# Batch 2's input load, first norm and first queries moved up in a hand-written instruction order

## The reference

```
x: (8, 512, 256);  mod = silu(c) @ wmod -> sa, ca, ga, sb, cb, gb per batch (ga, gb kept at least 0.25 from 0)
h = layernorm(x) * (1 + ca) + sa
x = x + ga * causal_attention(h, 16 heads of width 16)          # first attention
h = layernorm(x) * (1 + cb) + sb
xn = layernorm(h) * ln_g + ln_b
o = full_attention(xn, 32 heads of width 8) @ wo + h            # second attention
y = gelu(o @ w1[e] + b1[e]) @ w2[e] + b2[e]                     # an expert for each 256 tokens
out = x + gb * y
```

## Time and profile before

| | |
|---|---|
| time, median of 3 runs | 1482.61 us (1480.02 to 1482.8) |
| the profiled execution: time / its span | 1480.15 us / 1478.4 us |
| PE, DVE, ACT, POOL busy | 94%, 76%, 68%, 33% of the span |
| main steps 0, 4, 8, 12, 16 start (PE) | 60.42, 73.69, 87.72, 100.68, 113.77 us |
| granted TensorE clock | 0.999 |

### The profile page before, as it was taken

One profiled execution on the slowest core, in us unless ns is written; L12 is line 12 of the kernel. 1 busy time (PEld: TensorE's weight loads), 2 busy tenths in 40 slices (PEclk: granted clock), 3 DMA queues, 4 the chain that ended last, 5 costly groups with the idle time before them and its releaser, 6 DMA issues.

```text
span 1478.4 us, 29822 instructions
## 1 busy us (share of the span) xinstructions
PE 1395.2 (94%) x9588; PEld 592.0 (40%) x9588; DVE 1124.9 (76%) x2850; ACT 1007.1 (68%) x2094; POOL 489.2 (33%) x1242
## 2 busy tenths in 40 slices
PE   8888899998999999999999999999999989999998
PEld 5333333332443344433434334343344333343337
DVE  6777889988687878789687886868867797867721
ACT  4256567887767776767767676776766766786772
POOL 3345555332331434224341433415333133302100
PEclk9999999999999999999999999999999999999999
DMA  7776545545372645547365453735537341535240
GB/s 226 192 182 175 125 129 150 171 133 130 104 211 78 192 118 149 146 135 184 96 180 142 131 146 101 215 113 155 135 97 204 92 117 43 165 93 156 91 130 15
DMA packets 193887, 204.97 MB, mean 139 GB/s; under 512 B 58432, under 2 KB 143744, under 8 KB 193736
## 3 DMA queue, kind: packets, MB, share of 16 engines
q1 hardware_dynamic: 189960, 200.53, 49.9%
q10 hardware_dynamic: 3776, 2.53, 0.6%
HBM read 123.99 MB, written 79.02 MB: 137 GB/s over the span
## 4 chain that ended last, share of the span: by engine, by line
PE 76%; DVE 9%; ACT 8%; issue 3%; DMA 2%; SPq 1%; POOL 1%; ACTq 0%; DVEq 0%; POOLq 0%
PE bank_out L1596 18%; PE bank_scores L1574 14%; PE bank_max L1552 10%; PE bank_side L1513 8%; PE bank_side L1693 7%; PE bank_side L1526 4%; PE bank_max L1673 4%; ACT probs L1348 3%; DVE max_column L1822 3%; PE bank_side L1673 2%; PE bank_side L1634 2%; PE bank_scores L1673 2%; DVE bank_max L1819 2%; PE bank_side L1646 2%; ACT L1348 1%
## 5 line engine op out<-in xcount | busy, mean ns | idle before, releaser
L1348 ACT ACTIVATE probs<-bank_scores 128x512 f32<-128x512 f32 (+3 forms) x1536 | 753.1, 544 | 269.6 <-PE bank_scores L1574 264.0
L1822 DVE TENSOR_REDUCE max_column<-bank_max 128x1 f32<-128x512 f32 x1024 | 653.1, 682 | 96.0 <-PE bank_max L1552 91.7
L1596 PE MATMUL bank_out<-probs,v_tile 128*9 128x512 f32 (+4 forms) x3072 | 361.6, 542 | 5.4 <-ACT probs L1348 1.6
L1574 PE MATMUL bank_scores<-q_stack,k_stack 64*128 64x512 bf16 (+3 forms) x2048 | 313.9, 343 | 31.9 <-ACT probs L1348 29.7
L1552 PE MATMUL bank_max<-k_stack,q_stack 64*128 64x512 bf16 (+3 forms) x2048 | 308.4, 336 | 23.2 <-DVE max_column L1819 10.3
L1819 DVE CUSTOM_DVE_ANT_0 bank_max<-bank_max,causal 128x384 f32<-128x384 f32 (+3 forms) x512 | 241.8, 515 | 108.1 <-PE bank_max L1552 104.8
L1574 PEld LDWEIGHTS bank_scores<-q_stack,k_stack 64*128 64x128 bf16 x2048 | 81.0, 93 | 421.1 <-issue 415.2
L1178 POOL CAST max_parts<-max_row 128x32 bf16<-128x32 f32 x96 | 22.8, 237 | 386.9 <-DVE max_row L1835 386.0
L1552 PEld LDWEIGHTS bank_max<-k_stack,q_stack 64*128 64x128 bf16 x2048 | 101.8, 94 | 94.0 <-issue 60.6
L1693 PE MATMUL bank_side<-w_out,hidden_T 128*128 128x256 f32 x448 | 126.5, 405 | 0.0
L1196 POOL TENSOR_SCALAR_AFFINE_SELECT probs<-probs 128x512 f32<-128x512 f32 x128 | 81.6, 637 | 77.4 <-ACT probs L1348 76.8
(11 more groups left out here) (158 smaller groups left out, 1369.2 us busy)
## 6 DMA issues: line engine op xcount, KB each, us to landing
q_stack<-q_parts SPq DMA_DIRECT2D x124, 256.0 KB, 4.4
k_stack<-k_parts SPq DMA_DIRECT2D x124, 192.0 KB, 5.9
out_raw<-out_raw SPq DMA_DIRECT2D x74, 256.0 KB, 2.7
w_in<-in_L_ffn_w_dram SPq DMA_DIRECT2D x15, 1024.0 KB, 5.2
w_out<-in_L_ffn_w_dram SPq DMA_DIRECT2D x15, 1024.0 KB, 7.2
q_parts<-partsq SPq DMA_DIRECT2D x32, 384.0 KB, 3.1
k_parts<-partsk SPq DMA_DIRECT2D x32, 384.0 KB, 3.5
q_parts<-partsq SPq DMA_DIRECT2D x32, 256.0 KB, 3.1
```

The costliest lines, as they stand in the source:

```text
L1348: nc.scalar.activation(probs[s % 2][:, head_at(k), q0:S], region[bank][:, q0:S], ACT.Exp, scale=float(WIDTH[a]) ** -0.5).then_inc(drained[ ...
L1574: ins = pe.matmul(region[to][:, q0:S], k_stack[buf][rows, at, kt * P:(kt + 1) * P], q_stack[buf][rows, at, q0:S], start=(i == 0), stop=last)
L1596: ins = pe.matmul(outb[32 * k:32 * k + WIDTH[a] + 1, q0:S], v_tile[a][:, kt, g * GROUP + k, :], probs[s % 2][:, k, q0:S], start=(kt == 0), ...
L1822: v.tensor_reduce(dst, region[bank], AX_X, ALU.max).then_inc(drained[bank], 1)
```

## The change

Batch 2's `load_x` goes from slot 3 of the causal steps into the opening. Its norm up to the second of three Newton steps goes into the last slots of the lead-in, its normalising to slots 5 and 7 of the causal steps (the pieces stood in slots 7 to 27). Its two transposes go from slots 29 and 33 to 9 and 13, and its eight `qk` items from slots 37 to 65 to slots 17 to 45. No item is added or taken away.

```diff
@@ -438,13 +438,15 @@
-    second = [*v_items(0, 0), ("stacks", 0, 0), ("stacks", 0, 1), *norm_1[NEWTON_PIECE + 1:], *features_items(1, 0), ("idle_products", 0, 102), *qk_items(0, 1)[:4]]
+    second = [*v_items(0, 0), ("stacks", 0, 0), ("stacks", 0, 1), *norm_1[NEWTON_PIECE + 1:], *features_items(1, 0), ("load_x", 2), ("idle_products", 0, 102), *qk_items(0, 1)[:4]]
...
     place_at(beside, (20, 22, 24, 26), v_items(0, 1))
+    place_at(beside, (20, 22, 24, 24, 24, 24, 24), layernorm_items(2, 0)[:NEWTON_PIECE + 1])
+    place(beside, 27, [("newton", 2, 0, 1)])
@@ -457,14 +459,13 @@
     place_at(beside, (54, 88), [("blanks", 1, 0), ("blanks", 1, 1)])
-    place(beside, 3, [("load_x", 2)])
     place(beside, 10, [("stacks", 1, 0)])
     place(beside, 39, [("stacks", 1, 1)])
     place(beside, 40, [("load_gate", 0)])
-    place_norm(beside, (7, 10, 14, 15, 15, 15, 15, 25, 27), 2, 0)
-    place_at(beside, (19, 23), [("newton", 2, 0, 1), ("newton", 2, 0, 2)])
-    place_at(beside, (29, 33), features_items(2, 0))
-    place_at(beside, (37, 41, 45, 49, 53, 57, 61, 65), qk_items(0, 2))
+    place_at(beside, (5, 7), layernorm_items(2, 0)[NEWTON_PIECE + 1:])
+    place(beside, 0, [("newton", 2, 0, 2)])
+    place_at(beside, (9, 13), features_items(2, 0))
+    place_at(beside, (17, 21, 25, 29, 33, 37, 41, 45), qk_items(0, 2))
```

## The result

The changed kernel takes 1488.15 us (median of 5, 1486.64 to 1488.66) against 1482.43 (1480.02 to 1482.8): a ratio of **1.0043, 95% interval 1.0032 to 1.0053**. It is slower by 0.4%, 5.7 us where +1.1 was forecast, and outside the range. The profiled execution took 1488.52 us with a span of 1486.8.

The account below looks back on a forecast made before the run. PE's work was taken as the bound on average, with SP's queue and trip landings setting some steps. Step 16's +1.7 us (opening's 0.8 included) less 0.6 gave +1.1 us: 1483.7 us, 8-in-10 range 1479.9 to 1486.8.

Parts of the forecast that it names:

- Part 1, the load in the opening, +0.8: Opening: x_in ahead of trip 0's load on the full queue delays step 0 to 61.2 us, +0.8 us (0 to 1.4).
- Part 2, the norm, 0: Lead-in: some 2.5 us of norm work on DVE fits where DVE waits for PE, cost 0.
- Part 3, five products earlier: Steps 0 to 16: five qk fill PE's idle time; step 8 at 88.5, step 12 at 102.0, PE ready at 112.3.
- Part 4, the queue behind trip 2: SP's queue after trip 2: 2.49 MB instead of 0.92 delays trip 4's load to 113.7, step 16 to 115.5, +1.7 us.
- Part 5, steps 16 to 20, -0.6: Steps 16 to 20: one qk of 1.06 us leaves step 16, about half gained, -0.6 us (0 to -1.06).
- The rival of the clock (0.08): PE's clock falls to 1.2 GHz after the new 3.2 us wait before step 16: +4.3 us, 1486.9 us; chance 0.08.
- the queue is slower: Queue behind trip 2 runs at 275 GB/s, 9.1 instead of 6.8 us: +3.4 us in all, 1486.0 us; chance 0.12.

Follow-up runs that it names:

- kernel 2: The changed kernel with SP issuing batch 2's four stores of split queries and keys at their old slots, products still early: 1480.89 us, ratio 0.9996.
- kernel 3: The changed kernel with only the second two of batch 2's four part stores back at their old slots 57 and 65: 1482.33 us, ratio 1.0006.
- kernel 1: The kernel before with only batch 2's x_in load moved into the opening: 1483.02 us against 1481.92, ratio 1.0010.
- kernel 4: The changed kernel with the gate and bias loads (384 KB) moved from slot 40 to 66, behind trip 4's load: 1487.55 us, ratio 1.0036.
- kernel 6: The changed kernel with 22 matmuls of zeros on PE between steps 15 and 16: 1486.61 us, ratio 1.0034.
- kernel 5: The changed kernel with batch 2's four early part stores issued by ACT on its own queue, three slots behind the products: 1483.44 us, ratio 1.0015.
- 9: Kernel 2 with six more zero products on PE ahead of step 0: 1481.31 us, ratio 1.0002.
- 10: Kernel 8 with six more zero products on PE ahead of step 0: 1482.41 us, ratio 1.0002.
- kernel 7: Kernel 2 with batch 2's x_in load put ahead of batch 0's stack loads in SP's queue: 1480.26 us, ratio 0.9993.
- kernel 8: Kernel 2 with batch 2's x_in load in the opening issued by ACT instead of SP: 1481.26 us, ratio 0.9993.

## Why the prediction was wrong

**Direction, place and mechanism of the wait were right; its size was not, and the fall of the clock behind it was left out of the sum.** The forecast said +1.1 us, from a new wait before step 16 that the four early stores make through SP's queue. Kernels 2 and 3 show that chain. At step 20 the profile is some 6 us later than forecast: 1.0 from the opening, -0.9 from steps 0 to 12, 3.4 from steps 12 to 16 and 2.4 from steps 16 to 20.

- *Part 1, the load in the opening, +0.8.* The times of kernel 1 give +1.1 us, within its ends, but with an interval of 0.1 to 2.7. In the profile it is +1.8, from two sizes: trip 0's load went out at 59.93 and not at 59.4, and from that load to step 0 it takes 2.2 to 2.3 us in all ten profiles in which PE waits for it, not the 1.8 taken over from trip 2. So the slack before step 0 was 0.3 to 0.4 us and not 0.8.
- *Part 2, the norm, 0.* `x_in` landed at 53.0 us, and DVE's first statistic ran at 54.23. Nothing waited.
- *Part 3, five products earlier.* Step 8 was due at 88.5 and came at 89.0, step 12 at 102.0 and came at 102.09. That this fits is luck: the opening was 1.0 us late, and steps 0 to 8 and 8 to 12 took 0.5 and 0.4 us less than forecast. The text had step 8 still waiting for trip 2; it was PE's own work that set it (12.68 of 13.00 us busy, no wait for the trip). Steps 12 to 16 want 11.8 to 11.9 us (the changed kernel up to its wait, kernel 2), not 10.3, so PE was ready at 113.9 and not 112.3. Four items of 1.06 us taken away give back 13.09 - 11.9 = 1.2 us of 4.2; PE now waits in between for ACT's exponentials and DVE's maxima, 0.3 to 0.6 us at a time.
- *Part 4, the queue behind trip 2: the step that failed.* Trip 4's load was due at 113.7 and went out at 117.09, 3.4 us later. Of these, 1.0 is the opening and 0.7 is trip 3, whose load was due at 96.3 and went out at 98.04. The other 1.6 lie where the text says "From there to trip 4's store the order has the same bytes" and takes over the 15.1 us of the kernel before from the stack loads to trip 4's load; 16.7 passed (100.35 to 117.09). Two things in those 15.1 us did not carry over. Before, SP reached the store at 102.0 and waited until 103.5 for its rows, so 1.5 us of a delay should have vanished there; but SP now took 1.2 us longer to issue what stands between, the whole stretch without a pause. And the trip itself was taken at 5.7 us and took 7.6, of which 1.9 are the slower issue of its store. The second store of queries, put in just ahead of the stack loads and counted only with its 1.6 us of issue, had 768 KB in flight there, and kernels 3 and 4, with fewer bytes ahead of the trip, had it sooner. But how much of the 1.6 us these bytes are is open: kernel 2, with the order of before from trip 3 to trip 4, took 16.6 us for the same stretch, and the others with that order 15.9 to 16.8. The 15.1 of the one profile read is the shortest of them. The rate was not what failed: 0.7 us on the 6.8 of trip 3's 2.49 MB is about 330 GB/s (an estimate from these times), inside the bounds of 275 and 367. The rival *the queue is slower* named a trip 4 after 115 as its sign, and the sign came, but not from that stretch.
- *Part 5, steps 16 to 20, -0.6.* At full clock they take 14.59 instead of 14.99 in kernels 2, 3 and 6: -0.4.
- *The rival of the clock (0.08) came true beside the forecast.* It was priced at +3.2 us, and is 2.25 us (kernel 6). The wrong thing was the chance, and that it was treated as a case apart: the text forecast a wait of 3.2 us, and in kernel 4 the clock fell behind one of 3.03 us. With this term in the sum the forecast would have been some +3.4 us (1.1 + 2.25). The Trainium skill's rule cited there (TensorE: Matmul & The Clock Gate, Part 1) agrees with the rows at these waits: the same four matmuls took 1.03 us instead of 0.61 after 3.03 and 5.08 us of waiting, and 0.61 after 1.14 us. A single wait of PE does not explain all falls, though: in kernel 5 the clock fell with no wait above 0.95 us near it, and from 60 to 76 us it fell behind waits of 0 to 2.1 us (9 and 10).

The loss in the profiles by the parts: opening +1.8, steps 0 to 12 -0.4, the wait +3.8, the clock and step 16's missing product +1.85, together +7.1 at step 20. In the times, by the ratios of the kernels: the load +1.0 thousandths, the early norm and products -1.4, the first two stores +1.0, the second two +3.7 with the clock in it. The sum is +4.3, as measured, because it is made of the same ratios. The first has 0.9 of uncertainty, the others 1.2 to 1.4, so the first two stores' part alone is not shown by the times.

A version that surely beats the kernel before was not found. Kernels 7 and 8 have the lowest ratios, 0.9993, with 1 inside both intervals.

## What to carry to other kernels

When work that ends in a store is moved up, the store moves up in the issuing engine's order as well, and a round trip of a few KB behind it pays. Ask for each small transfer when its data are ready and when the issuing engine comes to it: here it came 4.5 us late, and that was most of the loss. Or move the products and leave the stores, as kernel 2 does. Take such a stretch from several profiles: the same order took 15.1 to 16.8 us. And where a forecast holds a new wait of PE of some 3 us, the fall of the clock after it belongs in the sum and not among the rivals.

## What the hardware showed that was not expected

- SP's issue can itself be slow: three stores of 8 KB each took 4.20 us and 5.70 us to issue (kernel 6) with the DMA share at 1.08, against 1.62 us with the share at 0.06 (trip 1). Whatever SP has next waits too. A full share alone does not tell it: trip 3's stores took 1.63 us with the share at 1.09.
- An engine that computes pays for its transfers with its own time: 1.9 us for two of ACT's, and PE waited 1.52 us.
- With nearly the same order, the clock from 60 to 76 us read between 0.68 and 1.00, and the time of four steps went from 13.8 to 16.2 us. Six zero products in the wait before it did not hold it up.
